# A routed feed-forward stage: second expert matrix read in place by TensorE, expert numbers loaded once per half, a result slot for every tile, one rectified block of four on VectorE

## What is computed

```python
x = x + 0.5 * _L0_ffn_ref(_layernorm(x), ...)     # attention, then 8 experts, one per token
x = x + _L0_attn_ref(_layernorm(x), ...)          # causal attention
x = x + 0.5 * _L0_ffn_ref(_layernorm(x), ...)     # the first step again
x = x + 0.5 * _L1_ffn_ref(x, ...)                 # dense
x = x + _L1_attn_ref(x, ...)                      # causal attention
x = x + 0.5 * _L1_ffn_ref(x, ...)                 # dense again
```

```python
logits = hn2 @ gate_w + gate_b
idx = jnp.argmax(logits, axis=-1)
mid = jax.nn.relu(jnp.einsum('th,ehf->etf', hn2, w1) + b1[:, None, :])   # 128 -> 512
y = jnp.einsum('etf,efh->eth', mid, w2) + b2[:, None, :]                 # 512 -> 128
moe = y[idx, jnp.arange(hn2.shape[0])]
```

## Time and profile before

| what | value |
|---|---|
| median of three runs | 1014.93 us |
| profiled execution, its own time | 1020.19 us |
| its span, first to last instruction | 1018.4 us |
| busy in the span | PE 88%, DVE 77%, ACT 66%, POOL 34% |
| mean granted TensorE clock | 0.966 of full |
| chain that ended last | PE 53%, DVE 21%, issue 10%, ACT 10% |

### The profile page before, as it was taken

How to read it: one execution, slowest core, us unless ns; L and a number is a source line. 1 busy time by engine, 2 the same in 40 slices (tenths; PEclk the granted TensorE clock), 3 DMA queues, 4 the chain that set the end, 5 groups by cost and what they waited for, 6 DMA issues and landing times.

```text
span 1018.4 us, 25342 instructions
## 1 busy us (share of the span) xinstructions
PE 897.5 (88%) x10020; PEld 477.1 (47%) x10020; DVE 779.7 (77%) x1412; ACT 674.8 (66%) x1470; POOL 342.2 (34%) x603
## 2 busy tenths in 40 slices
PE   2699999898778799999899999889698989999998
PEld 1123333236767455554323333249685645555465
DVE  5889899855447887888989999817368788888646
ACT  2288887786555577777798878786362358767631
POOL 4444312242646323233232312516571133311100
PEclk8599999999989899999999999999799989999999
DMA  5117740001133221121010200010310222110000
GB/s 146 46 44 178 191 107 2 16 10 47 43 94 85 78 66 35 35 66 43 23 46 22 55 11 2 23 41 30 97 33 24 62 64 65 33 38 4 3 22 21
DMA packets 60520, 52.29 MB, mean 51 GB/s; under 512 B 9106, under 2 KB 57362, under 8 KB 60402
## 3 DMA queue, kind: packets, MB, share of 16 engines
q1 hardware_dynamic: 48980, 40.00, 14.6%
q10 hardware_dynamic: 8478, 4.62, 2.2%
q0 software_dynamic: 2944, 6.05, 1.8%
HBM read 13.64 MB, written 11.06 MB: 24 GB/s over the span
## 4 chain that ended last, share of the span: by engine, by line
PE 53%; DVE 21%; issue 10%; ACT 10%; another core or an unknown queue 2%; DMA 2%; POOL 1%; DVEq 1%; ACTq 0%; SPq 0%; POOLq 0%
PE ps L576 14%; PE ps L652 13%; DVE negm L937 10%; ACT pt L770 7%; PE ps L715 4%; PE ps L607 3%; PE ps L707 3%; PE ps L701 3%; PE ps L582 3%; DVE blockm L928 2%; PE ps L721 2%; PE ps L660 2%; PE ps L612 1%; PE ps L670 1%
## 5 line engine op out<-in xcount | busy, mean ns | idle before, releaser
L770 ACT ACTIVATE pt<-ps 128x512 f32<-128x512 f32 (+1 forms) x896 | 458.3, 567 | 156.1 <-PE ps L576 107.2
L937 DVE TENSOR_REDUCE negm<-ps 128x2 f32<-128x1024 f32 x256 | 300.9, 1219 | 31.0 <-PE ps L576 28.4
L652 PE MATMUL ps<-pt,va 128*32 128x256 f32 (+1 forms) x4352 | 274.3, 341 | 12.1 <-ACT ot L776 5.5
L928 DVE TENSOR_REDUCE blockm<-ps 128x8 f32<-128x1024 f32 (+1 forms) x192 | 195.2, 1042 | 34.2 <-PE ps L576 21.8
L576 PE MATMUL ps<-ks,qs 61*128 61x128 bf16 (+2 forms) x1536 | 174.0, 293 | 35.7 <-DVE negm L937 16.0
L576 PE MATMUL ps<-qs,ks 64*128 64x128 bf16 (+3 forms) x1408 | 168.1, 296 | 7.8 <-ACT pt L770 2.3
L652 PEld LDWEIGHTS ps<-pt,va 128*32 128x32 f32 x4352 | 91.9, 108 | 124.5 <-issue 83.0
L576 PEld LDWEIGHTS ps<-ks,qs 61*128 61x128 bf16 x1536 | 54.8, 95 | 189.8 <-issue 86.6
L1206 POOL CAST mpart<-negm 128x16 bf16<-128x16 f32 x64 | 13.2, 207 | 300.2 <-DVE negm L937 153.8
L804 ACT ACTIVATE stage<-ps,pt 128x128 f32<-128x128 f32 x240 | 68.6, 373 | 41.6 <-PE ps L701 29.8
L1241 POOL DMA_INDIRECT y_rows<-pt,numbers_y x60 | 70.7, 1179 | 63.4 <-DVE pt L1058 55.0
(11 more groups left out here) (151 smaller groups left out, 1017.9 us busy)
## 6 DMA issues: line engine op xcount, KB each, us to landing
qs<-parts SPq DMA_DIRECT2D x80, 128.0 KB
ks<-parts SPq DMA_DIRECT2D x77, 128.0 KB
experts<-in_experts SPq DMA_DIRECT2D x8, 578.0 KB, 6.3
sorted<-stage ACTq DMA_DIRECT2D x4, 967.5 KB, 8.3
qs<-mrow SPq DMA_DIRECT2D x128, 6.0 KB
pt<-y_rows SPq DMA_DIRECT2D x8, 256.0 KB, 2.9
qs<-parts SPq DMA_DIRECT2D x32, 56.0 KB
ks<-parts SPq DMA_DIRECT2D x30, 56.0 KB
```

The lines of the kernel that those rows point to most:

```text
L652: ins = pe.matmul(pv_bank[32 * j:32 * j + 32, q0:q1], va[n % 2][:, kb, value_at(g, j):value_at(g, j) + 32], pt[:, k_, from_:from_ + q1 - q ...
L770: a.activation(pt[:, k_ % NPT, S * s:S * s + width], b_bank(o + s)[:, 0:width], ACT.Exp).then_inc(b_free, 1)
L928: v.tensor_reduce(blockm[:, g % 2, :, t, PLACES[c_]], pair_of(ka)[:, :, 0:width].rearrange("p s (b c) -> p s b c", c=P), AX, ALU.max, nega ...
L937: v.tensor_reduce(negm[:, g % 2, :, t, c_], pair_of(ka), AX, ALU.max, negate=True).then_inc(a_free, 1)
```

## The change

- The packed expert is reordered to w1, b1, b2, w2. `lay` copies only the first three, 128 x 644, and `we` has five slots for three. The matmuls of `dn` read w2 where it lies in `experts`, at an address that PE takes from a register.
- The 15 owners of a half are loaded by one instruction into 15 registers, each then checked: on DVE in `place` 2, where one was loaded, and once more on PE just ahead of the half's first `up`. The load at each `lay` goes.
- One of the four `up` matmuls becomes a job of its own, `uq`, of kind A, right behind `up`; DVE adds its bias and rectifies it into `mid_e`. ACT does three blocks.
- A result slot per tile (15 for 8); the copy of the token numbers goes, and POOL reads them in `sorted_rows`.
- The tables have other numbers, so that `lay`, some loads, projections, sums and dense jobs stand elsewhere. The first placement step of hm 1 now stands ahead of the scatter addresses. A new function asserts that routing steps stand in their order.

```diff
-NWE = 3
-NY = 8
+NWE = 5
+NY = SLOTS
+ON_DVE = 1
-WE = 2 * F + FB + P
+WE = F + FB + P
+W2_AT = WE
...
-TILES_AT = {0: {'start': 16.75, 'every': 0.207, 'lay0': 0.35, 'lay': 0.384, 'tt': -0.257, 'dn': 0.22699999999999998,
+TILES_AT = {0: {'start': 16.75, 'every': 0.207, 'lay0': 0.35, 'lay': 0.719, 'tt': -0.257, 'dn': 0.22699999999999998,
...
-                 (up, "up", hm, t), (up + T["dn"], "dn", hm, t), (up + T["ysend"], "ysend", hm, t)]
+                 (up, "up", hm, t), (up, "uq", hm, t), (up + T["dn"], "dn", hm, t), (up + T["ysend"], "ysend", hm, t)]
...
+        def experts_of(engine, hm):
+
+            k_ = SLOTS * (hm % 2)
+            return nc.values_load_multi_w_load_instructions(owner[0:1, k_:k_ + SLOTS], engines=[engine], min_val=0,
+                                                            max_val=E - 1)[1]
...
-                elif name == "up":
+                elif name in ("up", "uq"):
+                    if name == "up" and at == 0:
+                        need(pe, owner_step, 3 * n + 3)
+                        expert[n] = experts_of(mybir.EngineType.PE, n)
...
+                    need(pe, a_free, at_a[("uq", n, at)] + 1)
                     for a in range(FB):
+                        w2 = experts[:, bass.ds(expert[n][at], 1), W2_AT + a * P:W2_AT + (a + 1) * P]
                         ins = pe.matmul(pair_of(ka)[:, 0, 0:P], mid_e[:, number_of(n, at) % 2, a, :],
-                                        we[:, number_of(n, at) % NWE, F + a * P:F + (a + 1) * P], start=(a == 0),
-                                        stop=(a == FB - 1))
+                                        w2.rearrange("p o c -> p (o c)"), start=(a == 0), stop=(a == FB - 1))
...
-                    for fb in range(FB):
+                    for fb in range(FB - ON_DVE):
...
-                    next_expert[n] = expert_of(v, n, 0)
+                    expert[n] = experts_of(mybir.EngineType.DVE, n)
...
-                    v.tensor_copy(we[:, number_of(n, at) % NWE, :], experts[:, bass.ds(next_expert[n], 1), :]
+                    v.tensor_copy(we[:, number_of(n, at) % NWE, :], experts[:, bass.ds(expert[n][at], 1), 0:WE]
                                   .rearrange("p o c -> p (o c)")).then_inc(laid, 1)
-                    if at + 1 < SLOTS:
-                        next_expert[n] = expert_of(v, n, at + 1)
+                elif name == "uq":
+                    if tile_before(n, at, 2):
+                        need(v, a_full, at_a[("dn", *tile_before(n, at, 2))] + 1)
+                    for i in range(ON_DVE):
+                        fb = FB - ON_DVE + i
+                        bias = we[:, number_of(n, at) % NWE, F + fb:F + fb + 1]
+                        ins = v.tensor_scalar(mid_e[:, number_of(n, at) % 2, fb, :], a_tiles(ka)[:, i, :], bias, 0.0,
+                                              ALU.add, ALU.max)
+                    ins.then_inc(a_free, 1)
...
-                    v.tensor_copy(numbers_y[:, r:r + 1], sorted_rows[n % 2][:, at, P:ROW].bitcast(U32))
```

More of the change, by code:

```diff
@@ L120 @@
         11: {'lstats': 41.35, 'lrstd': 41.35, 'lnorm': 41.75, 'lT': 42.0}, 12: {'lstats': 5.662, 'lrstd': 5.615,
[L121 to L128, removed]
-        36.0}}
@@ L135 @@
[L135 to L142, removed]
@@ L143 @@
-NEXT_AT = {4: {'at': 20.651, 'stack': 0.801, 'every': 0.152}, 12: {'at': 41.47, 'stack': 0.801, 'every': 0.136}}
+        'lnorm': 6.3, 'lT': 6.8}, 13: {'lstats': 9.85, 'lrstd': 9.562, 'lnorm': 10.012, 'lT': 10.512}, 14:
+        {'lstats': 14.962, 'lrstd': 14.962, 'lnorm': 15.7, 'lT': 16.2}, 15: {'lstats': 17.65, 'lrstd': 17.48,
+        'lnorm': 17.88, 'lT': 18.13}}
+ROUTE_AT = {0: {'pick': 11.1, 'rank': 11.565, 'place0': 11.765, 'place1': 12.0, 'place2': 12.2, 'scatter': 12.209,
+        'every': 0.15, 'xload': 15.2}, 1: {'pick': 18.304, 'rank': 18.5, 'place0': 18.7, 'place1': 18.75, 'place2':
+        18.95, 'scatter': 18.8, 'every': 0.005, 'xload': 20.0}, 2: {'pick': 27.1, 'rank': 27.6, 'place0': 27.8,
+        'place1': 28.189, 'place2': 28.371, 'scatter': 28.3, 'every': 0.15, 'xload': 31.2}, 3: {'pick': 34.2,
+        'rank': 34.5, 'place0': 34.55, 'place1': 34.58, 'place2': 34.9, 'scatter': 34.362, 'every': 0.005, 'xload':
+        36.0}}
@@ new lines @@
+TILES_AT = {0: {'start': 16.75, 'every': 0.207, 'lay0': 0.35, 'lay': 0.719, 'tt': -0.257, 'dn': 0.22699999999999998,
+        'ysend': 0.277}, 1: {'start': 20.401, 'every': 0.207, 'lay0': 0.358, 'lay': 0.392, 'tt': -0.213, 'dn':
+        0.22699999999999998, 'ysend': 0.216}, 2: {'start': 32.628, 'every': 0.207, 'lay0': 0.35, 'lay': 0.304, 'tt':
+        -0.299, 'dn': 0.22699999999999998, 'ysend': 0.277}, 3: {'start': 36.033, 'every': 0.176, 'lay0': 0.329,
+        'lay': 0.215, 'tt': -0.257, 'dn': 0.22699999999999998, 'ysend': 0.508}}
@@ L146, in tiles_of @@
+NEXT_AT = {4: {'at': 20.651, 'stack': 0.803, 'every': 0.152}, 12: {'at': 41.47, 'stack': 0.801, 'every': 0.062}}
 def tiles_of(hm):
-    T, jobs = TILES_AT[hm], []
+    T, jobs, lay = TILES_AT[hm], [], -NEVER
     for t in range(SLOTS):
         up = T["start"] + T["every"] * t
-        jobs += [(up - (T["lay0"] if t < 2 else T["lay"]), "lay", hm, t), (up + T["tt"], "tt", hm, t),
-                 (up, "up", hm, t), (up + T["dn"], "dn", hm, t), (up + T["ysend"], "ysend", hm, t)]
+        lay = max(lay, up - (T["lay0"] if t < 2 else T["lay"]))
+        jobs += [(lay, "lay", hm, t), (up + T["tt"], "tt", hm, t),
+                 (up, "up", hm, t), (up, "uq", hm, t), (up + T["dn"], "dn", hm, t), (up + T["ysend"], "ysend", hm, t)]
@@ L167, in sums @@
 def sums(hm):
-    return [(Y_AT[hm][f"yadd{b}"], "yadd", 2 * hm + b, None) for b in range(2)]
+    Y = Y_AT[hm]
+    return [(max(Y["yadd0"], Y[f"yadd{b}"]), "yadd", 2 * hm + b, None) for b in range(2)]
 def norms(l):
@@ L247, in segment, with in_order @@
     return out
+ROUTING = [("gate", 0), ("gate", 1), ("pick", None), ("rank", None), ("place", 0), ("place", 1), ("place", 2)]
+COUNTED = ("lay", "tt", "up", "dn", "xfold", "yadd", "lstats", "lrstd", "lnorm", "stats", "rstd", "norm", "keep", "out")
+def in_order(plan):
+    at = {ev: i for i, ev in enumerate(plan) if ev[0] in ("gate", "pick", "rank", "place")}
+    steps = [("gate", 2 * hm + k, None) if name == "gate" else (name, hm, k) for hm in range(4) for name, k in ROUTING]
+    assert all(at[a] < at[b] for a, b in zip(steps, steps[1:]))
+    for name in COUNTED:
+        counted = [ev[1:] for ev in plan if ev[0] == name]
+        assert counted == sorted(counted, key=lambda ev: (ev[0], ev[1] or 0))
+    return plan
 def schedule(causal_of):
@@ L272, in schedule @@
         jobs += norms(12 + b) + dense(12 + b) + [(DENSE_AT[12 + b]["at"] + DENSE_AT[12 + b]["send"], "send", b, None)]
-    return plan + segment([12, 13, 14, 15], causal_of, jobs)
+    return in_order(plan + segment([12, 13, 14, 15], causal_of, jobs))
 def program(nc, d):
@@ L463, in program @@
                      "clear", "stack", "p1", "split", "m", "p2", "pv", "evac", "o", "onT", "out")
-        A_JOBS = ("p1", "v", "o", "out", "gate", "rank", "dn", "fu1", "fdn", "flip")
+        A_JOBS = ("p1", "v", "o", "out", "gate", "rank", "uq", "dn", "fu1", "fdn", "flip")
         B_JOBS = ("p2", "hT", "q", "k", "m", "onT", "lT", "tt", "up", "fu0")
@@ L849, in over_e @@
                 return t[:, :].rearrange("p (i o) -> p i o", o=1).broadcast_to([P, TILES, E])
[L851 to L856, removed]
+            expert = {}
             for ev in plan:
@@ L1275, in sync_program @@
                     elif n == 2:
-                        need(sp, a_free, at_a[("dn", 0, SLOTS - 1)] + 1)
+                        for r in range(NY):
+                            need(sp, y_sent[r], 16 * len(range(r, SLOTS, NY)))
                     else:
```

62 lines of the change are left out of this document (34 added, 28 removed).

## The result

The changed kernel takes 1048.51 us (1047.8 to 1049.35, four runs) against 1015.72 us of the kernel before in the same comparison: ratio 1.0323, 95% interval 1.0305 to 1.0341. It is slower by 32.8 us, where 7 were forecast, and the time lies above the range. The profiled execution has a span of 1046.6 us and a mean granted clock of 0.953, where it was 0.966.

A forecast was written before the change was run, and what follows sets the result against it. It took PE to set the pace in the routed stretches, with PE and DVE nearly full in attention. Costs of 19.5 us less gains of 12.4 gave +7.1 us over the median of 1014.93: 1022 us, range 1004 to 1036.

The forecast's parts named there:

- The sign: Whole kernel: the change makes it slower, chance 0.51, against 0.16 for same and 0.33 for faster.
- My own sum: Whole kernel: costs of 19.5 us less gains of 12.4 us, +7.1 us on the profiled execution.
- the block's length: Load of fifteen numbers with checks, on DVE or PE: 4.6 us, one load and fifteen checks of 0.283 us each.
- In hm 1 and 3 the first tiles wait for DMA and DVE anyhow: PE's blocks ahead of the first `up` of hm 1 and 3: covered by existing waits, counted as nothing.
- my terms for the blocks there and the clock: Blocks of hm 0 and 2: 8.2 us on PE, 7.7 us on DVE; half clock behind PE's idle time, 2.0 us.
- the clock, 2.0 us charged: PE returns at half clock after long idle time: one slow `up`, 1.0 us, charged twice.
- `uq` and the register instructions, 1.0 us charged: Routed tiles: `dn` needing this tile's `uq`, and 240 `dn` matmuls behind register instructions; 1.0 us, bounds 0 and 13.7.
- The gains, 12.4 us: Copy waits 7.9, sum ahead of layer norm 1.5, dense jobs ending hm 3 1.5, number copies on DVE 1.5 us.
- The rival of a cheap block: Blocks of fifteen numbers take 1.5 us, PE's clock does not fall: net -7.4 us, 1008 us, faster, chance 0.33.
- the one of no change: Blocks of fifteen numbers take 2.6 us: costs 11.45 against gains 12.4 us, 1014 us, chance 0.16.
- the rival of the long load: Every register pays its load: block 8.8 us, 1039 us, chance 0.08; milder form by the skill's figure, 7.25 us, 1032 us.
- The rival of the register instructions ahead of `dn`: Register instructions ahead of PE's `dn` matmuls all exposed: 13.7 - 1.0 us more, 1035 us, chance 0.05.

The follow-up runs named there:

- the run with both by tile: Changed kernel, but DVE and PE each load one number with its check per tile instead of blocks of fifteen: 1011.39 us, ratio 0.9960 to the kernel before.
- the chain of runs: Kernel before to changed kernel, part by part: 1015.6, matrix in place 1013.5, slots and placement step 1009.4, other due times 1002.4, `uq` 1011.4, blocks 1048.5 us.

## Why the prediction was wrong

The sign was right, and so was the mechanism: the load of the numbers "once per half" stands on the path, on DVE in attention and on PE ahead of the first `up`, the clock falls behind it, and the waits for the copy go. My own sum gave that sign a chance of only 0.51. Two steps failed.

The first is the block's length. I took 4.6 us, one load of 0.3 and fifteen checks at 0.283. The checks were right to a few per cent. The load is not one load's time: fifteen registers take 1.6 to 3.8 us. My bound of 8.8 us from the row of single loads, one load for each register, held this (up to 8.1), but I gave it a chance of 0.08 with the sentence that it is one instruction. The Trainium skill, page "Runtime: NRT & Kernel Launch", section "Instruction fetch mechanics", says about 200 ns per register even in bulk, beside its figure for the loads ahead of a kernel. The mean of the eight loads here agrees with 0.18 us, though no single load has it: 0.11 to 0.13 us a register in hm 0 and 2, 0.24 to 0.26 in hm 1 and 3. The four blocks that my sum counts, those of hm 0 and 2, took 6.0 us in the mean, and with that it gives 4 x 6.0 + 1.05 - 12.4 = +12.6: the length is worth 5.5 of the 25.7 us that I was short.

The second is the step "In hm 1 and 3 the first tiles wait for DMA and DVE anyhow [...] so I count nothing", and the same for DVE there. It left out four of the eight blocks. PE's waits for them in the changed profile are 7.72 and 7.15 us (DVE's) and 7.35 and 7.09 us (PE's). What they cost shows against the run with both by tile, which has no block. From the first `up` of hm 0 to that of hm 1 it takes 42.3 us and the changed kernel 52.4, from hm 2 to hm 3 40.9 and 53.7: 22.8 us where I counted nothing. With DVE's blocks alone these stretches are 8.6 us longer, with PE's alone 16.3. Up to the first `up` of hm 0, and from the last `dn` of hm 1 to the first `up` of hm 2, the changed kernel takes 22.5 us more; my terms for the blocks there and the clock give 4 x 6.0 - 2.55 + 2.0 = 23.4 with the measured length, so that part of the sum was right but for the 4.6. About 7 us come back in the rest of the run.

A cover has a length too: waits of 4 to 6 us can't hide two blocks of 8 us, and DVE's block came ahead of the wait that was to cover it, in the middle of hm 0's last tiles, while DVE was counted as half idle. One block alone did find cover: on the kernel before, DVE's made the same two stretches only 2.9 us longer. I had named the condition ("if that cover is gone each costs up to 4.6") and given it no chance of its own.

Of the other terms: the clock, 2.0 us charged for two drops; the trace has one behind each of the six stops in the routed parts, with eight matmuls at 1.91 to 2.05 us for 1.06. `uq` and the register instructions, 1.0 us charged: `uq` is 9.0 us as soon as nothing larger hides it, and 2.2 us here. The instructions ahead of `dn` take 46 ns each and PE's `dn` waits 4.5 us in twelve pieces for issue at its weight loads, so at most that much of their 11.0 us shows. The gains, 12.4 us, came to 13.2 us in the chain of runs (2.1 + 4.0 + 7.1); that the sums agree is in part luck, since no run separates the terms that I listed.

The rival of a cheap block and the one of no change are out by the same rows; the rival of the long load was the nearest by its mechanism, and its times of 1032 and 1039 us were short by the second step. The rival of the register instructions ahead of `dn` is out by the run with the matrix in place, which has them all and is not slower.

## What to carry to other kernels

Loading many registers at once is not one load: here each register cost 0.11 to 0.26 us and each bounds check 0.28, in one piece during which the engine's queue does nothing else. Small pieces beside work that is under way cost a fraction of it (120 single loads with checks: 37 us less than eight blocks). And before a cost is put at nothing because the engine waits there anyhow, compare the length of the cover with the length of the cost, and look at which comes first.

## What the runs showed that was not expected

- A load of fifteen registers takes 1.6 to 1.9 us in hm 0 and 2 and 3.5 to 3.9 us in hm 1 and 3, on both engines and in every run with blocks. Hm 0 and 2 read the numbers 0 to 14 of the row `owner`, hm 1 and 3 the numbers 15 to 29; the work beside them differs too, and which of the two makes the difference the runs don't show.
- PE's sequencer does a check in 0.146 us where DVE's takes 0.183, but with the gaps a number takes 0.28 to 0.29 us on PE and 0.28 on DVE, so the row of one engine was a fair bound for the other.
- The 120 single checks beside running work still cost 7.8 us, 0.065 us each.
